# DLRM tower: a new fixed order of a tile's steps on the engines, with a shorter way from a tile's first step to its last

## The reference

```python
e = stack([tbl_f[ids[:, f]] for f in range(26)], axis=1)      # 2048 x 26 x 64
x = layer_norm(dense @ Wd.T, gd, bd)                          # 2048 x 128
y = layer_norm(einsum('bnd,ed->bne', e, Ws), gs, bs)          # 26 features, 128 wide
y = layer_norm(einsum('bne,pn->bep', y, Wsi), gsi, bsi)       # mixed to 32 features
T = concatenate([x[:, None, :], swapaxes(y, 1, 2)], axis=1)   # 33 x 128
Zflat = einsum('bnd,bmd->bnm', T, T)[:, TRIL_I, TRIL_J]       # 528 pairs
z = layer_norm(Zflat @ Wl.T, gl, bl) * mask                   # 512 wide, the first 384 kept
h = maximum(concatenate([z, dense], axis=1) @ W_top1 + b_top1, 0.0)   # 768 -> 512
h = maximum(h @ W_top2 + b_top2, 0.0)                                 # 512 -> 256
out = h @ W_top3
```

## Time and profile before

| | |
|---|---|
| time, median of 3 runs (lowest, highest) | 616.3 us (614.75, 616.88) |
| span of the profiled execution | 614.1 us, 2.2 us under the median of the runs |
| TensorE busy | 526.2 us (86% of the span) |
| VectorE busy | 499.9 us (81%) |
| GpSimd busy | 400.5 us of gathers and 118.5 us between one gather's end and the next one's start |
| ScalarE busy | 339.1 us (55%) |
| granted TensorE clock, mean | 0.980 |
| last gather | starts at 529.25 us |

### The profile page before, as it was taken

One profiled execution on the slowest core, in us unless ns is written; L12 is line 12 of the kernel. 1 busy time (PEld: TensorE's weight loads), 2 busy tenths in 40 slices (PEclk: granted clock), 3 DMA queues, 4 the chain that ended last, 5 costly groups with the idle time before them and its releaser, 6 DMA issues.

```text
span 614.1 us, 17721 instructions
## 1 busy us (share of the span) xinstructions
PE 526.2 (86%) x6955; PEld 392.2 (64%) x6955; DVE 499.9 (81%) x977; ACT 339.1 (55%) x922; POOL 401.2 (65%) x422
## 2 busy tenths in 40 slices
PE   2458767789999998899999999999999998979877
PEld 1356546466766766576767676676767675756557
DVE  5597999979798989689898989898998988886510
ACT  3122536466675747375756566575747575755432
POOL 6777777777777777777777777777777777400000
PEclk9999889899999999899999999999999999999998
DMA  7311111111111111111111111112111111100000
GB/s 168 119 26 36 28 28 36 27 36 28 37 28 38 28 37 28 35 29 30 36 27 37 27 37 28 36 29 38 27 36 28 27 28 28 19 1 3 2 0 2
DMA packets 22611, 20.23 MB, mean 33 GB/s; under 512 B 12016, under 2 KB 14720, under 8 KB 22528
## 3 DMA queue, kind: packets, MB, share of 16 engines
q0 software_dynamic: 13312, 13.66, 12.5%
q1 hardware_dynamic: 8400, 4.33, 2.7%
q10 hardware_dynamic: 816, 1.11, 0.6%
HBM read 19.07 MB, written 0.01 MB: 31 GB/s over the span
## 4 chain that ended last, share of the span: by engine, by line
PE 38%; POOL 24%; issue 15%; DVE 10%; ACT 9%; DMA 4%; ACTq 0%; DVEq 0%; POOLq 0%
POOL emb L262 24%; PE b_l L404 7%; PE b_y L349 6%; PE b_l L421 6%; PE b_l L430 5%; PE b_z L361 5%; DMA emb<-in_tbl,idx 3%; ACT mixed L516 2%; DVE V L833 2%; DVE yb L815 2%; PE b_mix L337 2%; PE b_a L319 2%; DVE byn L810 2%; PE b_a L328 2%; DVE var_y L822 1%
## 5 line engine op out<-in xcount | busy, mean ns | idle before, releaser
L262 POOL DMA_INDIRECT emb<-in_tbl,idx x416 | 400.5, 963 | 128.2 <-issue 118.5
L521 ACT ACTIVATE sq<-yb 128x1024 f32<-128x1024 f32 x64 | 67.7, 1057 | 136.0 <-DVE yb L815 136.0
L815 DVE TENSOR_TENSOR yb<-b_y,bias_y 128x1024 f32<-128x1024 f32 x64 | 78.2, 1221 | 22.6 <-PE b_y L349 22.6
L349 PE MATMUL b_y<-mixed,projw 64*128 64x512 f32 x256 | 74.9, 663 | 23.5 <-ACT mixed L516 23.5
L833 DVE TENSOR_TENSOR V<-yb,rstd_y 128x256 f32<-128x256 f32 x256 | 91.9, 422 | 2.2
L822 DVE TENSOR_REDUCE var_y<-sq 128x32 f32<-128x1024 f32 x64 | 77.8, 1216 | 6.7 <-ACT sq L521 5.6
L404 PE MATMUL b_l<-wlt,zt 128*128 128x512 f32 x160 | 72.9, 602 | 0.8 <-issue 0.8
L328 PE MATMUL b_a<-gram_w,embt 128*128 128x128 f32 x416 | 67.1, 306 | 5.3 <-ACT embt L497 4.7
L337 PE MATMUL b_mix<-mix,byn 128*128 128x128 f32 x512 | 71.6, 285 | 0.0
L497 ACT ACTIVATE embt<-b_a 128x512 f32<-128x512 f32 (+1 forms) x64 | 33.0, 516 | 62.7 <-PE b_a L319 62.7
L337 PEld LDWEIGHTS b_mix<-mix,byn 128*128 128x128 f32 x512 | 65.5, 200 | 0.2
(11 more groups left out here) (132 smaller groups left out, 735.8 us busy)
## 6 DMA issues: line engine op xcount, KB each, us to landing
emb<-in_tbl,idx POOLq DMA_INDIRECT x416
dense<-in_r_dense_t SPq DMA_DIRECT2D x16, 128.0 KB, 2.1
V<-in_L_rec_Wl ACTq DMA_DIRECT2D x1, 1056.0 KB, 5.4
w<-in_W_top SPq DMA_DIRECT2D x2, 512.0 KB, 7.1
w<-in_W_top SPq DMA_DIRECT2D x1, 768.0 KB, 5.3
out_y<-y_sb SPq DMA_DIRECT2D x16, 0.5 KB
idx<-in_ids SPq DMA_DIRECT2D x1, 195.0 KB, 5.2
wd<-in_L_rec_Wd SPq DMA_DIRECT2D x1, 128.0 KB, 4.3
```

What stands on the lines that cost most here:

```text
L262: pool.indirect_dma_start(out=emb[t % 2][:, f, :], out_offset=None, in_=tables[f], in_offset=bass.IndirectOffsetOnAxis(ap=idx[:, t, f:f + ...
L349: last = nc.tensor.matmul(b_y[:, j2, :], projw[r, :], mixed[c % 2][r, :], start=True, stop=True, tile_position=(64 * j2, 0))
L815: nc.vector.tensor_tensor(yb[c % 2][:, :, :, :].rearrange("e h s p -> e (h s) p"), b_y[:, :, :].rearrange("e h (s p) -> e (h s) p", p=NP), ...
```

## The change

The counts of quarters are replaced by a stage of four parts `s` for each tile `t`, which also serves the tile behind it (`new = t + 1`, its measuring) and the tile ahead of it (`old = t - 1`, its interaction and dense layers). The four column steps run in `s = 0` to `s = 2`, with their last `scale` and `gram` in `s = 2` and `s = 3`. `by_sample`, `pair_rows` and the copies stand in `s = 3` of the same stage, `interact` of the tile in `s = 0` of the next, and the dense layers in its `s = 1` to `s = 3`: for a tile the pairs come 4 quarters sooner than before, the interaction 4 or 5, the dense layers 5 to 7 and the store 8, and there are 73 quarters where there were 81. On VectorE `add_bias` of the next column step stands ahead of `scale` of the last. The five parts of `prepare_wlt` are put into three quarters. The last rows of the pairs go through bank `b_l0` in place of `b_x` (`x_rows`, which waits for `copy_pairs`); some waits go, and `interact` waits for `copy_y` of the tile before. The gathers' counts of `gram_done` are set anew. The operations of a tile, their shapes and their number stay as they were.

In the listing the guards `if real(...)`, which skip tiles outside 0 to 15, and the removed lists of steps (they stand in the kernel above) are left out.

```diff
+LEAD = 5
+STORE = 12
+GATE = (1, 3, 4, 4)
...
+def stage(h):
+
+    t, s = divmod(h - LEAD, 4)
+    return t, t + 1, t - 1, s
...
-            after(pool, gram_done, 4 * t + b - PROJECT - 2)
+            after(pool, gram_done, 4 * (t - 2) + GATE[b])
...
     def dense_transposes(t):
...
-        after(pe, zt_copied, 2 * (t - 2))
...
     def pair_rows(t):
 
+        if t == 0:
+            pe.wait_ge(wlt_ready, RC)
         pe.wait_ge(zb_ready, 3 * (t + 1))
         after(pe, h1_relued, 4 * (t - 1) + 2)
         for c in range(4):
             last = nc.tensor.transpose(b_l0[:, c * P:(c + 1) * P], zb[:, ZB_PAIR + c * P:ZB_PAIR + (c + 1) * P], ident[:, :])
         last.then_inc(zt_done, 1)
-        pe.wait_ge(x_copied, 2 * min(t + 3, T))
-        nc.tensor.transpose(b_x[0:64, 0:P], zb[:, ZB_X:ZB_X + 2 * NP], ident[:, :], tile_position=(0, 0))
-        nc.tensor.matmul(b_x[64:96, 0:P], ones[:, 0:32], xt[t % 3][:, :], start=True, stop=True, tile_position=(0, 64)).then_inc(zt_done, 1)
+
+    def x_rows(t):
+        pe.wait_ge(zt_copied, 2 * t + 1)
+        nc.tensor.transpose(b_l0[0:64, 0:P], zb[:, ZB_X:ZB_X + 2 * NP], ident[:, :], tile_position=(0, 0))
+        nc.tensor.matmul(b_l0[64:96, 0:P], ones[:, 0:32], xt[t % 3][:, :], start=True, stop=True, tile_position=(0, 64)).then_inc(zt_done, 1)
 
     def interact(t):
-        if t == 0:
-            pe.wait_ge(wlt_ready, RC)
-        pe.wait_ge(zt_copied, 2 * (t + 1))
-        after(pe, h1_relued, 4 * t)
-        after(pe, h2_relued, 2 * (t - 1))
+        after(pe, y_copied, t)
         for c in range(RC):
+            if c == RC - 1:
+            pe.wait_ge(zt_copied, 2 * (t + 1))
             last = nc.tensor.matmul(b_l1[:, :], zt[:, c, :], wlt[:, c, :], start=(c == 0), stop=(c == RC - 1))
         last.then_inc(o_done, 1)
...
     def layer1(t, k):
...
-        if k == 1:
-            after(pe, y_copied, t)
...
     def layer2(t):
...
-        pe.wait_ge(z_ready, min(t + 2, T))
...
 @block.tensor
...
     for h in range(QUARTERS):
+        t, new, old, s = stage(h)
+        if s == 0:
+            transposes(new, 0)
+            interact(old)
+            norms(new, 0)
+            mix_features(t, 0)
+            project(t, 0)
+            mix_features(t, 1)
+        if s == 1:
+            project(t, 1)
+            transposes(new, 1)
+            interact_back(old)
+            mix_features(t, 2)
+            norms(new, 1)
+            gram(t, 0)
+            project(t, 2)
+            mix_features(t, 3)
+            dense_transposes(new)
+            layer1(old, 0)
+            dense_project(new)
+        if s == 2:
+            project(t, 3)
+            transposes(new, 2)
+            gram(t, 1)
+            layer1(old, 1)
+            norms(new, 2)
+            gram(t, 2)
+            layer2(old)
+        if s == 3:
+            gram(t, 3)
+            dense_back(new)
+            transposes(new, 3)
+            norms(new, 3)
+            layer3(old)
+            pair_rows(t)
+            x_rows(t)
...
-        if 5 <= h < 5 + RC:
-            prepare_wlt(h - 5)
+        if h in (5, 6):
+            prepare_wlt(2 * (h - 5))
+            prepare_wlt(2 * (h - 5) + 1)
+        if h == 7:
+            prepare_wlt(4)
...
-    def copy_zt(t):
+    def copy_pairs(t):
         act.wait_ge(zt_done, 2 * t + 1)
         after(act, o_done, t)
         nc.scalar.activation(zt[:, 0:4, :], b_l0[:, :].rearrange("p (c b) -> p c b", c=4), ACT.Copy).then_inc(zt_copied, 1)
+
+    def copy_x_rows(t):
         act.wait_ge(zt_done, 2 * t + 2)
-        nc.scalar.activation(zt[0:96, 4, :], b_x[0:96, 0:P], ACT.Copy).then_inc(zt_copied, 1)
+        nc.scalar.activation(zt[0:96, 4, :], b_l0[0:96, 0:P], ACT.Copy).then_inc(zt_copied, 1)
...
 @block.scalar
...
     for h in range(QUARTERS):
+        t, new, old, s = stage(h)
+        if s == 0:
+            copy_embt(new, 0)
+            deviation_o(old)
+            copy_mixed(t, 0)
+            square_y(t, 0)
+            scale_o(old)
+            copy_mixed(t, 1)
+        if s == 1:
+            deviation_y(t, 0)
+            copy_embt(new, 1)
+            square_y(t, 1)
+            copy_z(old)
+            copy_mixed(t, 2)
+            copy_zs(t, 0)
+            deviation_y(t, 1)
+            square_y(t, 2)
+            copy_mixed(t, 3)
+            deviation_n(new, 0)
+            copy_dt(new)
+        if s == 2:
+            deviation_y(t, 2)
+            relu1(old, 0)
+            copy_embt(new, 2)
+            square_y(t, 3)
+            copy_zs(t, 1)
+            relu1(old, 1)
+            deviation_x(new)
+            copy_zs(t, 2)
+            scale_x(new)
+            normalize(new, 0, 4)
+        if s == 3:
+            deviation_y(t, 3)
+            relu2(old)
+            normalize(new, 4, 7)
+            copy_zs(t, 3)
+            copy_x(new)
+            copy_embt(new, 3)
+            normalize(new, 7, 10)
+            deviation_n(new, 1)
+            copy_pairs(t)
+            normalize(new, 10, 12)
+            copy_x_rows(t)
+            copy_y(old)
...
 @block.vector
...
     for h in range(QUARTERS):
+        t, new, old, s = stage(h)
+        if s == 0:
+            normalize(t, 1)
+            shuffle(t)
+            norms(new, 0)
+            add_bias(t, 0)
+            recip_o(old)
+            variance(t, 0)
+        if s == 1:
+            add_bias(t, 1)
+            scale(t, 0)
+            norms(new, 1)
+            bound_n(new, 0)
+            variance(t, 1)
+            add_bias(t, 2)
+            scale(t, 1)
+            variance(t, 2)
+        if s == 2:
+            add_bias(t, 3)
+            scale(t, 2)
+            norms(new, 2)
+            variance(t, 3)
+            recip_x(new)
+            normalize(new, 0)
+        if s == 3:
+            scale(t, 3)
+            by_sample(t)
+            norms(new, 3)
+            bound_n(new, 1)
```

## The result

The new order takes 783.2 us (781.74 to 784.63, 4 runs) where the kernel before took 616.6 beside it: a ratio of 1.270, 95% interval 1.267 to 1.274, far outside the 0.3% that can be told. The forecast was 757 us, range 690 to 790. The profiled execution has a span of 781.1 us and a mean granted clock of 0.851.

A forecast was written before the change was run, and what follows sets the result against it. Before, 527 us of gathers and an 84 us drain; after, a ring of 40.0 us a tile. 61 + 44.3 + 560 + 43.1 = 708.4, plus 46.2 clock loss and 2.2 outside the span, gives 757 us, range 690 to 790.

The forecast's parts named there:

- The ring: Closed walk within a tile through three engine queues, by_sample ahead of the next normalize and shuffle on VectorE: 40.0 us a tile.
- GpSimd's long gaps that a `gram` ends: Sign on GpSimd's timeline: after the change the gathers, gapless before, would show long gaps ended by a gram.
- the waits at `zb`, `yb` and `prod`: Sign on VectorE: waits at zb for zs, yb for b_y, prod for b_a, each near its walked size.
- The clock's price: TensorE's loss from falling to 1.2 GHz behind two gaps a tile: 1.54 us each, 3.08 a tile, 46.2 in all.
- the first wait: TensorE's gap ahead of project(1), walked as 2.4 us standing still, with a clock loss of 1.54 us.
- the second wait: TensorE's gap ahead of gram(3), walked as 3.4 us standing still, with a clock loss of 1.54 us.
- clock lost longer: Rival: the second clock fall reaches into interact on TensorE, 5.3 us a tile, 790 us; chance 0.10.
- the forecast by itself: Whole kernel: the ring plus two clock losses a tile, 757 us, 735 to 775 by itself; chance 0.45.
- Wait (8): VectorE at norms of the next tile's first batch, behind interact, which waits for copy_y: 1.90 us.
- The ends: Outside the fourteen stages: first add_bias ends at 61, first stage 44.3, last tile's first add_bias to span's end 43.1 us.
- Edits costed at nothing: New gram_done counts, SyncE's earlier stores and dense loads, and dropped waits: claimed to cost nothing.

The follow-up runs named there:

- filled kernel: The new order with idle products in TensorE's four waits of a tile (ahead of project(1), gram(3), norms(new, 3), x_rows): 724.2 us.
- that run: New order with by_sample(old) behind shuffle(t), interaction and layers a stage later, four step swaps, norms(new, 3) ahead of gram(3), old gather counts: 646.3 us.
- the gate: The new order with the gathers' counts of gram_done as before, (0, 1, 2, 3) in place of (1, 3, 4, 4): 784.3 us.
- the second wait filled: The new order with idle products only ahead of gram(3), norms(new, 3) and x_rows, none ahead of project(1): 737.2 us.
- the first wait filled: The new order with idle products only ahead of project(1), nine of them: 751.8 us.

## Why the prediction was right, and where its sizes were off

**The ring** held. Walked as 40.0 us at full clock, it measured 40.4 with the clock held; its waits came to 10.85 walked and 10.64 in the filled kernel. GpSimd's long gaps that a `gram` ends, the waits at `zb`, `yb` and `prod`, and VectorE as the queue that closes the ring are all in the trace; opening it, with the other moves of that run, took a tile from 38.1 to 34.2 us.

**The clock's price** was mis-sized. The prediction took 1.54 us for each of two falls, 3.08 a tile, from one quarter behind one late gather. Measured are 1.02 behind the first wait and 2.87 behind the second. The second is the step that was off: it lies 8.5 us ahead of `interact`, and that the fall "reaches into `interact`", which stood in the rival of the longer loss with 5.3 a tile, is what happens, at 3.9 in all. The two errors have opposite signs and cancel in part, so that the sum is 3.08 for 3.9; that is luck. The 783 us lie outside the 735 to 775 of the forecast by itself, between it and the 790 of *clock lost longer*. Fourteen stages took 620.1 us for 14 x 43.08 = 603.1: 17.0 of the 26.5 us that are missing, 11 to 12 of them by the clock and the rest by the ring's 0.4.

**Wait (8)** was walked rightly for the full clock: in the filled kernel it is 1.62 us for 1.90, and `interact` starts at 424.61, 3.3 us behind `by_sample`'s end as walked and 0.05 us behind `copy_y`, which ends at 424.56. At the lower clock another neighbour holds it: in the new order `transposes(new, 0)` on TensorE's own queue keeps `interact` from 410.97 to 411.88, when `copy_y` had ended at 411.50.

```profile
411.25 0.25 ACT L633 ACTIVATE y_sb<-b_l 1x128 f32<-1x128 f32 x1
```

**The ends** were 9.5 us short: the first `add_bias` ended at 62.6 for 61; the first stage took 49.4 for 47.4, with the clock; and from the last tile's first `add_bias` to the end it was 49.0 for 43.1. In that last part no clock loss had been counted, and there were three falls: `project(2)` took 2.08 us, `interact` 6.16, and half of `layer1` ran at the lower level.

**Edits costed at nothing** cost nothing where it was tried: the gate (784.3 for 783.2). The bias ahead of the scaling was not costed by itself; undoing it costs 50 us in this order, those of a third fall of the clock among them. The stores and loads on SyncE were not tried alone.

The rule of the Trainium skill, page "TensorE: Matmul & The Clock Gate", section "HAM oscillation — how this bites in real kernels", that a loop with a long wait in each round falls back to the low clock in every round, holds in every tile of the new order: `interact` takes 5.76 us or more in each of the sixteen (4.56 at full clock), and holding the clock by idle products gave back 59 us. It does not hold of each wait: with the second wait filled, the first, 2.28 us in every tile, has no fall behind it in some of them.

## What to carry to other kernels

In static queues the time of a tile is the longest closed walk through them, not the busiest engine: VectorE had 29 us of work in either order, and the time went from 33 to 40 at full clock and to 44 with its falls. Before tightening a pipeline, find the step of this tile that stands ahead of a step of the next on the same engine, and walk from it back to itself, each queue's other tenants included. A reorder has no sign of its own: the same exchange of two instructions gained 50 us in one order and lost 35 in the other. And a wait of 2 to 3 us on TensorE can be charged twice, once as a wait and once as slower products behind it; what the second costs depends on whether a long product on the path comes before the clock is back.

## What the runs showed of the hardware

The length of a fall was not tied to the code. With the first wait filled, the same wait ahead of `gram(3)` was followed by 10.2 us at the lower level in one tile, from 1.9 us behind `gram(3)`'s start on, and by 6.8 us in the next, from 0.8 us ahead of it on. In the kernel after, where ten tiles in a row have the one length of 44.3 to 44.4 us, it is the long form each time by that length, 10.2 us in the tile shown. And 28 products a tile whose results nobody reads made the kernel 59 us faster.
